# A gated attention and FFN kernel: keys of tile 1 through another bank, sums of the last tiles reordered, the last FFN tile in halves

## The reference, cut to what matters

```python
q = instance_norm(layernorm(x)); k = instance_norm(ctx)
qp = Wq @ q + bq;  kp = Wk @ k + bk;  sp = Ws @ ctx + bs
attn = softmax(qp.T @ kp, axis=-1)              # 512 x 512 per batch
mean = sp @ attn.T;  mean_sq = (sp * sp) @ attn.T
std = sqrt(relu(mean_sq - mean * mean))
x = x + tanh(g_xattn) * (instance_norm(ctx) * std + mean)
w = (weight_q - 8) * scales + zeros             # 512 x 512, groups of 128
x = x + tanh(g_ffn) * (layernorm(x) @ w.T)
```

## Time and profile before

| | us |
|---|---|
| median of 3 runs | 179.69 (179.33 to 180.91) |
| the profiled execution, its own time | 180.87 |
| its span | 178.7 |
| TensorE busy | 164.8 |
| VectorE busy | 136.8 |
| GpSimd busy | 131.4 |
| ScalarE busy | 123.3 |

### The profile page before, as it was taken

One profiled execution on the slowest core, in us unless ns is written; L12 is line 12 of the kernel. 1 busy time (PEld: TensorE's weight loads), 2 busy tenths in 40 slices (PEclk: granted clock), 3 DMA queues, 4 the chain that ended last, 5 costly groups with the idle time before them and its releaser, 6 DMA issues.

```text
span 178.7 us, 2695 instructions
## 1 busy us (share of the span) xinstructions
PE 164.8 (92%) x832; PEld 108.1 (60%) x832; DVE 136.8 (77%) x277; ACT 123.3 (69%) x268; POOL 131.4 (74%) x155
## 2 busy tenths in 40 slices
PE   6768596999999999999999999999999999998992
PEld 6335473756667566656666575667656546866881
DVE  2899757776699779977987997777567579999941
ACT  2439737787788888778778887796889987723410
POOL 1407729656969997998899799996889899994100
PEclk9999969999999999999999999999999999999999
DMA  5991013005000400310000000000000000101323
GB/s 167 354 397 72 0 44 133 4 2 176 0 0 4 178 0 0 109 71 0 2 4 2 0 0 0 0 4 0 0 0 2 0 0 4 54 5 71 129 97 117
DMA packets 4717, 9.83 MB, mean 55 GB/s; under 512 B 480, under 2 KB 608, under 8 KB 4704
## 3 DMA queue, kind: packets, MB, share of 16 engines
q1 hardware_dynamic: 4704, 9.67, 14.9%
HBM read 7.57 MB, written 2.10 MB: 54 GB/s over the span
## 4 chain that ended last, share of the span: by engine, by line
PE 69%; DVE 14%; POOL 8%; ACT 5%; issue 2%; DMA 1%; ACTq 0%; POOLq 0%
PE pv_bank L285 25%; PE score L261 13%; PE turn_bank L271 13%; PE proj_bank L295 5%; ACT probs L399 3%; DVE X L687 2%; PE score L362 2%; POOL CTX L858 2%; DVE neg_max L560 2%; DVE stats L692 2%; PE score L358 2%; PE score L359 2%; DVE probs_t L711 2%; DMA X<-in_x 1%; POOL rstd L862 1%
## 5 line engine op out<-in xcount | busy, mean ns | idle before, releaser
L768 POOL TENSOR_SCALAR probs<-probs,rden 128x512 f32<-128x512 f32 x64 | 51.8, 815 | 12.1 <-DVE rden L565 12.1
L285 PE MATMUL pv_bank<-probs_t,values 128*128 128x512 f32 x120 | 58.8, 594 | 0.4 <-ACT VAR L417 0.4
L399 ACT ACTIVATE probs<-score,neg_max 128x512 f32<-128x512 f32 x64 | 44.3, 692 | 18.7 <-DVE neg_max L560 18.7
L560 DVE TENSOR_REDUCE neg_max<-score 128x2 f32<-128x1024 f32 x32 | 38.6, 1209 | 3.9 <-PE score L261 3.9
L271 PEld LDWEIGHTS turn_bank<-ident,probs 128*128 128x128 f32 x256 | 30.7, 142 | 16.1 <-issue 13.6
L408 ACT COPY probs_t<-turn_bank 128x512 f32<-128x512 f32 x64 | 37.4, 586 | 2.5 <-PE turn_bank L271 2.5
L271 PE MATMUL turn_bank<-ident,probs 128*128 128x128 f32 x256 | 36.3, 275 | 0.9 <-ACT probs_t L408 0.9
L285 PEld LDWEIGHTS pv_bank<-probs_t,values 128*128 128x128 f32 x120 | 19.4, 191 | 8.8 <-issue 8.8
L261 PE MATMUL score<-k_hi,q_hi 64*128 64x512 f32 x64 | 14.7, 450 | 5.8 <-DVE k_lo L554 3.6
L565 DVE RECIPROCAL rden<-den 128x1 f32<-128x1 f32 x64 | 9.6, 151 | 10.5 <-ACT probs L399 10.2
L261 PEld LDWEIGHTS score<-k_hi,q_hi 64*128 64x128 f32 x64 | 6.1, 183 | 18.0 <-issue 10.8
(11 more groups left out here) (85 smaller groups left out, 298.3 us busy)
## 6 DMA issues: line engine op xcount, KB each, us to landing
X<-in_x SPq DMA_DIRECT2D x8, 256.0 KB, 5.3
raw_ctx<-in_context SPq DMA_DIRECT2D x8, 256.0 KB, 2.7
sz<-in_scales_zeros SPq DMA_DIRECT2D x4, 512.0 KB, 3.7
out<-probs_t SPq DMA_DIRECT2D x8, 256.0 KB, 2.0
w_int<-in_weight_q_t SPq DMA_DIRECT2D x1, 1024.0 KB, 8.3
params_sb<-in_params SPq DMA_DIRECT2D x1, 226.0 KB, 3.9
```

The lines of the kernel that those rows point to most:

```text
L285: mm = pe.matmul(sums_bank(t, b)[:, :], values[t % 2][:, i, b, :, :].rearrange("p a c -> p (a c)"), probs_t[t % 2][b][:, i, :], start=(i = ...
L399: act.activation(probs[c % PROBS][:, :], score[g % 2][:, N * b:N * b + N], ACT.Exp, bias=neg_max[:, g % 4, b:b + 1], accum_out=den[:, g % ...
L560: dve.tensor_reduce(neg_max[:, g % 4, :], score[g % 2][:, :].rearrange("p (b m) -> p b m", b=2), AX_X, ALU.max, negate=True).then_inc(max_ ...
L768: pool.tensor_scalar(probs[c % PROBS][:, :], probs[c % PROBS][:, :], rden[:, g % 4, b:b + 1], 1.0, ALU.mult, ALU.mult).then_inc(probs_done, 1)
```

## The change

- Head: the keys of tile 1 are projected into `pv_bank`, between the first turn and `scores(3)`. ScalarE keeps them one step earlier, VectorE takes the statistics of ctx(1) ahead of the first maximum, and keeps k_lo(1) right behind `maximum(3)`.
- In odd steps, `weigh(.., 3)` goes ahead of the second turn.
- The sums of (6, 1) and (7, 1) use `proj_bank`, those of (6, 0) and (7, 0) `pv_bank` (before: only (7, 0) used `proj_bank`).
- For tiles 6 and 7 the square of the mean is made by ScalarE from PSUM inside `keep_sums`, not by GpSimd. `mean_sq` is still one buffer, so the first half waits until the variance before has been taken (`var_done`).
- `root(1)` is moved into the last but one step. Of the last group of weights, the zeros' addition and the remainder are done by VectorE instead of GpSimd.
- `with_mean(7)` is moved one FFN tile on. The last FFN tile is computed, added and stored in two halves of 256 columns.

```diff
         def k_bank(t):
-            return pv_bank if t == 0 else proj_bank
+            return pv_bank if t < PLAIN else proj_bank
         def sums_bank(t, b):
-            return proj_bank if (t, b) == (TILES - 1, 0) else pv_bank
+            return proj_bank if b == 1 and t >= TILES - 2 else pv_bank
...
-            for u in range(TILES):
+            for u in range(TILES - 1):
                 sp.wait_ge(result_done, u + 1)
                 sp.dma_start(out_tiles[u], result[u % 4]).then_inc(stored[u % 4], DMA)
+            for h in range(2):
+                u = TILES - 1
+                cols = slice(h * N // 2, (h + 1) * N // 2)
+                sp.wait_ge(result_done, u + 1 + h)
+                sp.dma_start(out_tiles[u][:, cols], result[u % 4][:, cols]).then_inc(stored_half[h], DMA)
...
                 if t > 0:
-                    pe.wait_ge(q_lo_done, t + 1)
+                    pe.wait_ge(k_lo_done, t)
                 pe.matmul(k_bank(t)[:, :], w_qk[:, 1, :], CTX[:, t, :], start=True, stop=True).then_inc(k_done, 1)
...
                     pe.wait_ge(s_squared, t + 1)
-                    if sums_bank(t, b) is proj_bank:
-                        pe.wait_ge(s_kept, t + 1)
-                    elif (t, b) == (0, 0):
-                        pe.wait_ge(k_lo_done, 1)
+                    if (t, b) == (0, 0):
+                        pe.wait_ge(k_lo_done, PLAIN)
+                    elif (t, b) == (TILES - 2, 1):
+                        pe.wait_ge(s_kept, TILES)
+                    elif t == TILES - 1:
+                        pe.wait_ge(sums_kept, 4 * t + 2 * b - 2)
                     else:
-                        pe.wait_ge(sums_kept, min(2 * (2 * t + b), 4 * (TILES - 1)))
+                        pe.wait_ge(sums_kept, 4 * t + 2 * b)
                 mm = pe.matmul(sums_bank(t, b)[:, :], values[t % 2][:, i, b, :, :].rearrange("p a c -> p (a c)"),
...
             turn(0, 0)
+            project_k_plain(1)
             scores(3)
             turn(0, 1)
-            project_k_plain(1)
             turn(1, 0)
...
                         weigh(t - 1, j // 2, 2)
+                        weigh(t - 1, j // 2, 3)
                     turn(g, 1)
-                    if t > 0 and j % 2 == 1:
-                        weigh(t - 1, j // 2, 3)
                     if t > 0 and j % 2 == 0:
...
                 last.then_inc(y_turned, 1)
+
+            def feed_forward_halves(u):
+                pe.wait_ge(yt_hi_done, u + 1)
+                pe.wait_ge(yt_lo_done, u + 1)
+                pe.wait_ge(result_done, u - 2)
+                for h in range(2):
+                    cols = slice(h * N // 2, (h + 1) * N // 2)
+                    for g in range(GROUPS):
+                        hi = yt_hi[u % 2][:, P * g:P * g + P]
+                        pe.matmul(ffn_bank[(u + h) % 4][:, cols], hi, w_hi[:, g, cols], start=(g == 0), stop=False)
+                        pe.matmul(ffn_bank[(u + h) % 4][:, cols], hi, w_lo[:, g, cols], start=False, stop=False)
+                        mm = pe.matmul(ffn_bank[(u + h) % 4][:, cols], yt_lo[u % 2][:, P * g:P * g + P],
+                                       w_hi[:, g, cols], start=False, stop=(g == GROUPS - 1))
+                    mm.then_inc(ffn_done, 1)
...
             pe.wait_ge(ffn_lo_done, GROUPS)
-            for u in range(TILES):
+            for u in range(TILES - 1):
                 feed_forward(u)
...
                     turn_y(u + 2)
+            feed_forward_halves(TILES - 1)
...
                     act.wait_ge(mean_added, t - 1)
-                    act.wait_ge(mean_squared, t - 1)
+                    act.wait_ge(mean_squared, min(t - 1, TILES - 2))
                 act.copy(MEAN[t % 2][half(b), :], sums_bank(t, b)[0:C, :]).then_inc(sums_kept, 1)
+                if t >= TILES - 2:
+                    if b == 0:
+                        act.wait_ge(var_done, t)
+                    act.activation(mean_sq[half(b), :], sums_bank(t, b)[0:C, :],
+                                   ACT.Square).then_inc(half_squared, 1)
                 act.copy(VAR[half(b), t, :], sums_bank(t, b)[C:P, :]).then_inc(sums_kept, 1)
...
                     keep_turned(g, 0)
-                    if g == 1:
+                    if g == 0:
                         keep_k_hi(1)
...
                         root(0)
+                        root(1)
...
-            root(1)
             root(2)
...
+            def add_zeros(g):
+                dve.wait_ge(w_scaled, g + 1)
+                dve.tensor_tensor(w_deq[g % 2][:, :], w_deq[g % 2][:, :], sz[:, g, 1, :],
+                                  ALU.add).then_inc(w_deq_done, 1)
+
+            def remainder(g):
+                dve.wait_ge(ffn_hi_done, g + 1)
+                dve.tensor_tensor(w_lo[:, g, :], w_deq[g % 2][:, :], w_hi[:, g, :].bitcast(F32),
+                                  ALU.subtract).then_inc(ffn_lo_done, 1)
+
             def weights_hi(g):
...
             normalise_x(1)
+            ctx_statistics(1)
+            ctx_variance(1)
+            maximum(0)
+            ctx_shifted(1)
+            maximum(1)
+            reciprocal(0, 0)
+            normalise_ctx(1)
+            reciprocal(0, 1)
...
                         scale_weights(t - TILES + 4)
+                    if j == 1 and t == TILES - 1:
+                        add_zeros(3)
                     if j == 2 and t >= TILES - 2:
                         weights_hi(t - TILES + 4)
+                    if j == 3 and t == TILES - 1:
+                        remainder(3)
                     if j == 0 and t >= 2:
...
                 dve.wait_ge(scaled_done, u + 1)
+                dve.wait_ge(mean_added, u + 1)
                 dve.scalar_tensor_tensor(X[:, u, :], CTX[:, u, :], tanh_g[:, 0:1], X[:, u, :],
...
             finish_statistics(4)
+            def add_ffn_half(u, h):
+                cols = slice(h * N // 2, (h + 1) * N // 2)
+                dve.wait_ge(ffn_done, u + 1 + h)
+                dve.wait_ge(stored[u % 4], DMA * (u // 4))
+                dve.scalar_tensor_tensor(result[u % 4][:, cols], ffn_bank[(u + h) % 4][:, cols], tanh_g[:, 1:2],
+                                         X[:, u, cols], ALU.mult, ALU.add).then_inc(result_done, 1)
+
             for u in range(TILES):
+                if u == TILES - 1:
+                    add_ffn_half(u, 0)
+                    add_ffn_half(u, 1)
+                    break
                 add_ffn(u)
...
                     keep_y_lo(u + 2)
-                if u == 0:
-                    with_mean(TILES - 1)
                 if u + 5 < TILES:
...
                     relu(TILES - 1)
+                if u == 1:
+                    with_mean(TILES - 1)
...
             def variance(t):
-                pool.wait_ge(mean_squared, t + 1)
+                if t < TILES - 2:
+                    pool.wait_ge(mean_squared, t + 1)
+                else:
+                    pool.wait_ge(half_squared, 2 * (t - TILES + 3))
+                    pool.wait_ge(sums_kept, 4 * (t + 1))
                 pool.tensor_tensor(VAR[:, t, :], VAR[:, t, :], mean_sq[:, :], ALU.subtract).then_inc(var_done, 1)
...
             x_deviation(1)
+            ctx_deviation(1)
             normalise_probs(0, 0)
             normalise_probs(0, 1)
-            ctx_deviation(1)
             normalise_probs(1, 0)
...
                         weights_lo(2)
-                    if j == 1 and t == TILES - 1:
-                        dequantise(3)
-                    if j == 2 and t == TILES - 1:
-                        weights_lo(3)
...
             inverse_deviation2(2)
-            square_mean(TILES - 2)
             variance(TILES - 2)
...
             inverse_deviation2(4)
-            square_mean(TILES - 1)
             variance(TILES - 1)
```

More of the change, by code:

```diff
@@ L115, in gated_attention_ffn @@
         stored = [sem(f"stored{i}") for i in range(4)]
+        stored_half = [sem(f"stored_half{h}") for h in range(2)]
         power_ready = sem("power_ready")
@@ L623, in _ @@
             reciprocal(1, 1)
-            normalise_ctx(1)
             keep_q_lo(1)
```

15 lines of the change are left out of this document (5 added, 10 removed).

## The result

| | before | after |
|---|---|---|
| median, us (four runs each) | 179.73 (179.33 to 180.91) | 182.78 (181.94 to 183.14) |
| profiled execution, its own time | 180.87 | 182.87 |
| its span | 178.7 | 181.1 |

The changed kernel takes 1.0154 times the time of the kernel before, 95% interval 1.0104 to 1.0203: slower, by about 3 us in the medians.

The account below looks back on a forecast made before the run. TensorE's own work was taken to bound the kernel from 30.40 to 133.70 us. From 180.87: -2.4 head, +2.1 late FFN start (3.6 - 1.5), +1.4 clock, -0.3 end gave 181.67, stated as 181.6; range 178.8 to 183.1.

Parts of the forecast that it names:

- The head: Before 30.4 us: projecting tile 1's keys earlier gives -2.4 us, about 1.4 from the half-clock stretch, 1.0 from order.
- The middle: Odd steps, second value product ahead of the turn: same TensorE work, 0 us, bounds 0 to +0.3.
- The bank of (6,1): Before the FFN: sums of (6,1) in proj_bank remove a 0.42 us wait, given back by ScalarE's added Square and root(1).
- The new wait: ScalarE's Square of (7,0) waits for variance(6), y_hi(0) behind it: FFN starts +3.6 us later, bounds +2.8 to +4.2.
- The waits absorbed: Inside the FFN: 1.5 us of TensorE waits vanish because the late start lets VectorE and GpSimd get ahead.
- The clock behind the pause: FFN start: TensorE's pause of about 3.7 us brings a clock fall, +1.4 us, bounds 0 to 2.4.
- The end: Last FFN tile in halves: matmuls +0.2, shorter last addition and transfer, together -0.3 us, bounds -0.7 to +0.3.
- that the clock holds: Rival: the clock stays up behind the long pause ahead of the FFN, 180.2 us, within 1%; chance 0.2.
- That the wait isn't there in effect: Rival: variance(6) is done when the Square of (7,0) comes up, so the kernel is faster, 178.5 us; chance 0.12.
- The third: Rival: the clock falls in the head as well, or the halves run at the weights' load pace, 183.0 us; chance 0.13.

Follow-up runs that it names:

- squares on GpSimd: Changed kernel with the squares of the means of tiles 6 and 7 back on GpSimd, without the ScalarE Square and its wait: 178.42 us, ratio 0.992 to before.
- two buffers: Changed kernel with two mean_sq buffers, for even and odd tiles, so the Square of (7,0) waits only for variance(5): 178.72 us, ratio 0.990 to before.
- y ahead: Changed kernel with y_hi(0), y(2) and y_hi(1) ahead of the sums of (7,0) on ScalarE, still one mean_sq buffer: 178.05 us, ratio 0.989 to before.
- the pause was filled: Changed kernel with 14 extra unused matmuls of 128 columns in TensorE's pause ahead of the FFN: 180.57 us, ratio 1.002 to before.
- pause in the head filled: Kernel before with 7 extra unused matmuls of 128 columns in the 1.93 us pause ahead of scores(4): 179.74 us, ratio 0.997 to before.

## Why the prediction came out as it did

The direction and the mechanism were right, and the measured 182.78 lies 1.2 above the predicted 181.6, within the range and 0.3 below its upper end. The loss of over 1% that came had been given no more chance (0.45) than no clear difference. In the profiled execution's own time the forecast was +0.8 and the trace has +2.0. By its steps:

- **The head**, -2.4: -2.62. scores(4) at 19.46 for 19.35, scores(5) at 20.65 for 20.85. The clock held there in the changed kernel's profile and in all runs of the head alone. The prediction took it as held while calling it not safe, and rightly so: one profile of the new head (squares on GpSimd) shows the fall.
- **The middle**, 0: 0, by its own run too.
- **The bank of (6,1)**, 0.4 gained and given back: the order of ScalarE came as worked out. The wait of 0.42 us became one of 0.32 for the values, and the weighing of (7,0) starts at 138.02, which is 140.64 with the head's 2.62 put back, against 140.65 before. No run has it alone.
- **The new wait**, which the prediction put at the center: there as described, at the Square of (7,0), released by GpSimd's variance(6), with y_hi(0) behind it, 2.31 us for the 2.5 foreseen. Both ways of taking it away (two buffers, y ahead) turn the loss into a gain, and so does taking out the Square. The size was +4.26 for +3.6. This is the term "+3.6 us" that was mis-sized, by 0.66: y_hi(0) came at 149.69, which is 152.31 with the head's 2.62 put back, where 151.65 stood in the prediction. The prediction's upper bound named "0.6 of contention more"; the rows have it in VectorE's addition of 1.74 us, on which the deviations and GpSimd's whole row up to variance(6) depend: with the 2.62 put back the first deviation starts 1.40 later than before (141.37 against 142.59), where the prediction had its chain 0.6 late.
- **The waits absorbed**, -1.5: -1.37, the FFN has none for q_lo. The work alone was put at 25.1 and is 25.29, since the two tiles without a turn take 2.88 and 2.97. The waits come back when the FFN starts early: with y ahead 1.46 us of TensorE's idle time, 1.96 when counted as the 1.37 is, by the FFN's length less its work.
- **The clock behind the pause**, +1.4: 2.2 by the runs, 2.6 by the profile, at the top of its bounds or 0.2 above. The step that failed was to take the amount "as in the head". There 3.30 us at half clock had done 1.65 us of work. Here the clock stayed low for about 6.9 us by its mean of 0.52 over 7.18, and the whole first tile with its turn (3.24 us of work) fell into it. The fall's length in the head was no measure of it: of the changed kernel's four runs three have a mean clock of 0.981, which is again about 6.9 us, and one 0.991, which is about 3.3 us as in the head; that one is the fastest, at 181.94.
- **The end**, -0.3: +0.04 for the matmuls where +0.2 stood (24 of them, 0.119 apart), -0.55 for addition and transfer, which were put at -0.5, and -0.40 more around the span, which the prediction had not counted. In all -0.91 in this profile; the halves alone measure 0.8 to 0.9 us within either set.

The misses, +0.8 at the FFN's start with its waits, +1.2 for the clock, -0.6 at the end and -0.2 in the head, make the 1.2 between +0.8 and +2.0. A further 1.0 between the difference of own times (2.0) and of medians (3.05) is that the profile of before was one of the executions with the fall in the head, as the prediction supposed from the spread of the three times.

The rivals: that the clock holds (180.2) came true only where the pause was filled, at 180.57. That the wait isn't there in effect (178.5) fell with the row of the Square, and the relief of GpSimd on which it counted was undone in one kernel without a loss beyond its scatter. The third, 183.0, was closer in time than the forecast itself, but not in its cause: the clock held in the head of the profiled execution and the halves did not slow down.

## What to carry to other kernels

When an operation is given to another engine to relieve the first, look at the one buffer that both still share: the wait for it now stands in the second engine's row, and costs what is queued behind it. Before paying for another buffer, see whether the late waiter can stand behind the work that the bounding engine needs next; three calls moved past one took the same loss away as a second buffer. And when a profile is read for a difference of 1%, run the kernel often enough to see whether its times fall into two sets, and which of them the profiled execution is from.

## What the runs showed of the hardware

- The same pause of 1.93 us, between the same instructions of the head, was followed by a granted clock of 0.50 in one profiled execution (the kernel before) and by 1.00 in two (the halves alone, the middle alone). In the kernel before, over three groups of runs, 33 of 61 executions held the clock, and the two sets are 1.2 us apart. A pause of 1.20 us was followed by the fall in two profiled executions (squares on GpSimd; pause in the head filled) and in the others not. Behind 4.16 us the clock fell in the profiled execution, and all four runs of the changed kernel have a mean clock below 1.00: three at 0.981 with 182.68 to 183.14 us, one at 0.991 with 181.94.
- The fall came about a microsecond into the dense work behind a pause of 1.75 us (matmuls of 0.40, then 0.63), but some 1.1 us ahead of it where the pause was 4.16 us long (0.88 in the mean of the last 4.52 us before the FFN).
- A VectorE addition of two inputs in SBUF took 1.74 us instead of 0.75 beside two GpSimd operations back to back.
- Storing the last result in two halves made not only the transfer shorter (1.7 instead of 2.0 us) but also what lies around the span: 1.77 us in the kernel after and 1.82 to 1.99 in the runs with only the halves, against 2.1 to 2.2 in the kernel before.
- A matmul of 256 columns in fp32r costs half of one of 512 (0.119 us apart against 0.23), so splitting the last tile cost TensorE almost nothing.
